# Layer 0 of a two-layer gated transformer: the slot schedule of its attention rewritten on all four engines, and the first steps of the last feed-forward reordered

## The reference

```
x = x + tanh(g_xattn[0]) * xattn0(layernorm(x), ctx)     # 16 heads of 16, 77 keys, this is "layer 0" below
x = x + tanh(g_ffn[0])   * moe(layernorm(x))             # 8 experts, top 2
x = x + tanh(g_xattn[1]) * xattn1(layernorm(x), ctx)     # 16 heads of 64
x = x + tanh(g_ffn[1])   * ffn(layernorm(x))             # amax of the input, quantize, gelu, amax of hidden, quantize

def xattn0(query, key_value):
    q, k, v = heads(query @ Wq + bq), heads(key_value @ Wk + bk), heads(key_value @ Wv + bv)
    attn = softmax(clip(q @ k.T / sqrt(16), -1e4, 1e4))
    return merge(attn @ v) @ Wo + bo
```

## Time and profile before

| | |
|---|---|
| median of 3 runs | 1161.29 us (1160.04 to 1161.42) |
| the profiled execution | 1163.3 us, of which the span from first to last instruction 1161.2 us |
| layer 0's attention in the span | 0 to about 246 us |
| the last feed-forward in the span | about 1015.6 us to the end |
| busy share of the span | TensorE 91%, VectorE 79%, ScalarE 72%, GpSimd 46% |

### The profile page before, as it was taken

The page is one execution under the profiler, slowest core; times in us unless marked ns, Lnnn a source line. Parts: engine busy times, 40 slices in busy tenths (PEclk is TensorE's granted clock), DMA queues, the critical chain, the costliest instruction groups (busy, mean ns, idle before and its releaser), DMA issues.

```text
span 1161.2 us, 26321 instructions
## 1 busy us (share of the span) xinstructions
PE 1057.4 (91%) x8919; PEld 775.3 (67%) x8919; DVE 916.9 (79%) x1960; ACT 834.7 (72%) x2382; POOL 539.4 (46%) x515
## 2 busy tenths in 40 slices
PE   6888888868969999999999999589999999889898
PEld 5666666645537777777777777357777777645477
DVE  5999999957845687666666667479999999789798
ACT  4988889836656456556556667378888888569896
POOL 5888888732252122122122111178889887500140
PEclk9999999979989999999999999889999999989899
DMA  6443334349672343333333335345252423010034
GB/s 150 118 128 110 110 110 133 123 128 284 189 206 61 53 137 90 118 101 121 124 104 120 121 115 161 112 127 161 68 158 67 154 74 92 28 38 0 1 119 137
DMA packets 128814, 132.12 MB, mean 114 GB/s; under 512 B 24792, under 2 KB 112973, under 8 KB 128557
## 3 DMA queue, kind: packets, MB, share of 16 engines
q1 hardware_dynamic: 119901, 112.17, 32.0%
q0 software_dynamic: 6480, 17.70, 5.5%
q10 hardware_dynamic: 2304, 0.59, 0.3%
HBM read 82.78 MB, written 47.64 MB: 112 GB/s over the span
## 4 chain that ended last, share of the span: by engine, by line
PE 57%; DVE 4%; ACT 4%; issue 2%; DMA 1%; POOL 1%; DVEq 0%; SPq 0%; ACTq 0%; POOLq 0%
PE exp_ps_h L1527 15%; PE exp_ps_y L1540 9%; PE a_ps_o L1953 9%; PE a_ps_sc L1937 8%; PE f_ps_h L2264 5%; PE exp_ps_y L1546 5%; PE a_ps_p L1924 3%; ACT exp_h L1590 2%; DVE f_hlo L2395 2%; PE exp_ps_x L1506 1%; PE f_ps L2447 1%; PE f_ps L2443 1%; PE f_ps_x L2255 1%; DVE all_xn L2404 1%; PE a_ps_x L1911 1%
## 5 line engine op out<-in xcount | busy, mean ns | idle before, releaser
L1590 ACT ACTIVATE exp_h<-exp_ps_h,exp_b_now 128x256 f32<-128x256 f32 (+1 forms) x320 | 124.7, 440 | 142.4 <-PE exp_ps_h L1527 142.4
L1491 POOL DMA_INDIRECT exp_xg<-xn,all_token_of x71 | 84.4, 1188 | 304.0 <-PE exp_ps_x L1506 288.5
L1527 PE MATMUL exp_ps_h<-exp_xhi,exp_w_now 128*128 128x256 bf16 (+1 forms) x1280 | 196.4, 263 | 5.9 <-DVE exp_xlo L1625 5.9
L1986 ACT ACTIVATE a_z<-a_ps_sc,a_nmx 128x77 f32<-128x77 f32 x512 | 159.3, 367 | 35.6 <-DVE a_nmx L2088 35.6
L1527 PE MATMUL exp_ps_h<-exp_xlo,exp_w_now 128*128 128x256 bf16 (+1 forms) x640 | 161.4, 263 | 0.0
L1703 DVE TENSOR_TENSOR exp_hlo<-exp_h,exp_hhi 128x512 bf16<-128x512 f32 (+1 forms) x160 | 99.4, 632 | 70.4 <-ACT exp_hhi L1597 68.5
L1540 PE MATMUL exp_ps_y<-moe_w2s,exp_hhi 128*128 x568 | 134.2, 379 | 1.3 <-DVE exp_y L1722 1.3
L1527 PEld LDWEIGHTS exp_ps_h<-exp_xhi,exp_w_now 128*128 128x128 bf16 x1280 | 120.6, 99 | 20.7 <-issue 8.3
L1986 ACT ACTIVATION_READ_ACCUMULATOR a_z<-a_ps_sc,a_nmx 128x1 f32 x512 | 127.0, 248 | 0.0
L1953 PE MATMUL a_ps_o<-a_v_now,a_phi 128*128 128x256 bf16 (+1 forms) x640 | 106.6, 272 | 2.3 <-DVE a_plo L2077 2.3
L1937 PE MATMUL a_ps_sc<-a_k_now,a_xhi 128*128 128x462 bf16 (+1 forms) x384 | 98.6, 341 | 3.4 <-DMA a_k_now<-fold_klo 2.2
(11 more groups left out here) (279 smaller groups left out, 2735.5 us busy)
## 6 DMA issues: line engine op xcount, KB each, us to landing
a_stage<-in_L_ffn_W_dram SPq DMA_DIRECT2D x64, 256.0 KB, 3.2
y_slots<-exp_y SPq DMA_DIRECT2D x71, 128.0 KB, 1.7
fold_k<-route_kst SPq DMA_DIRECT2D x16, 308.0 KB, 4.5
fold_v<-route_vst SPq DMA_DIRECT2D x16, 308.0 KB
exp_job_in<-fold_k SPq DMA_DIRECT2D x14, 352.0 KB, 3.3
exp_job_in<-fold_v SPq DMA_DIRECT2D x14, 352.0 KB, 3.3
a_x<-in_x_dram SPq DMA_DIRECT2D x32, 128.0 KB, 2.3
x<-a_xo SPq DMA_DIRECT2D x32, 128.0 KB, 1.7
```

The costliest lines, as they stand in the source:

```text
L1491: pool.indirect_dma_start(out=xg[:, v, u, :], out_offset=None, in_=xn_dram[:, :], in_offset=bass.IndirectOffsetOnAxis(ap=at.bitcast(U32), ...
L1527: mm = pe.matmul(hidden[:, i, f % 2, slots(j)], w1_now[:, v, k, hl, f * P:(f + 1) * P], xx[:, k, slots(j)], start=(q == 0), stop=(q == len ...
L1590: ins = act.activation(h[:, f, slots(j)], hidden[:, i, f % 2, slots(j)], ACT.Gelu_apprx_tanh, bias=b1_now[:, v, f:f + 1])
L1986: ins = act.activation(z[:, u, h * KEYS:(h + 1) * KEYS], ps_sc[:, j, (h - SB[j][0]) * KEYS:(h - SB[j][0] + 1) * KEYS], ACT.Exp, bias=nmx[: ...
```

## The change

In `attention`, what each engine does in slot T:

- TensorE turns x(T+1) first, then scores(T), then chunks 0 to 3 of tile T-2, output(T-3), queries(T+1), chunks 4 to 7, then the first part of the value products, chunks 8 and 9, and the other two parts. `part` cuts `turns` into three lists by the chunks they read: 7, 7 and 3 products. The queries are one slot ahead of their scores.
- ScalarE: ReLU and exponential, copy of chunks 0 to 3, queries(T+1), the other two copies, both splits, xn(T+2), attnT(T-2). The xn is a slot earlier than before, attnT too.
- VectorE: `turned` ahead of the largest, the largest ahead of xo.
- GpSimd: both remainders one slot later, at the slot's head and round `power`; the multiplication last.

In `ffn`: x's rounding starts before the reciprocal and the product that only the steps need (`steps_of` becomes `scale_of` and `step_of`); two products of group 0 come ahead of group 1's transposes; the constant for rounding is set in f1, and f3's first scaling starts before the output steps.

```diff
@@ attention @@
+    part = [[i for i in turns if blocks[i][0] // 4 == k] for k in range(3)]
@@ gpsimd, def slot @@
+                if has(T - 1):
+
+                    pool.wait_ge(s["hi_done"], 2 * T - 1)
+                    at, cols = (T - 1) // 2, slice(v * 512, (v + 1) * 512)
+                    pool.tensor_tensor(w1[:, at, 1, cols], stage[:, v, 0, :], w1[:, at, 0, cols],
+                                       ALU.subtract).then_inc(s["lo_done"], 1)
                 if has(T + 2):
                     power(T + 2, u)
+                if has(T - 1):
...
                 if has(T):
 
                     pool.wait_ge(s["xn_done"], T + 1)
                     pool.tensor_tensor(x[:, t, :], x[:, t, :], gbo[:, :], ALU.add).then_inc(s["xb_done"], 1)
-
-                    pool.wait_ge(s["hi_done"], 2 * T + 1)
...
@@ tensor @@
+            queries(0)
 
             def slot(T, t, b):
+                if has(T + 1):
+                    wait(pe, s["pT_done"], 3 * (T - 2))
+                    pe.wait_ge(s["qT_done"], T + 1)
+                    turn_x(T + 1)
                 if has(T):
                     pe.wait_ge(s["qT_done"], T + 1)
                     if t == 0:
@@ -454,40 +472,37 @@
                             mm = pe.matmul(ps_sc[:, j, g * PAIR:(g + 1) * PAIR], qT[lane, g, :], kblk[lane, b % 2, g, :],
                                            start=True, stop=True)
                     mm.then_inc(s["scores_done"], 1)
+                if T == 1:
+                    values(1, 0)
                 if has(T - 2):
                     if T == 2:
                         pe.wait_ge(s["kT_done"], 1)
+                    pe.wait_ge(s["norm_done"], T - 1)
+                    wait(pe, s["pT_done"], 3 * (T - 3) + 1)
+                    turn_p(T - 2, 0)
+                if has(T - 3):
+                    output(T - 3)
+                if has(T + 1):
+                    queries(T + 1)
+                if has(T - 2):
+                    wait(pe, s["pT_done"], 3 * (T - 3) + 2)
+                    turn_p(T - 2, 1)
+                    wait(pe, s["xo_done"], T - 2)
+                    if t == 2:
+                        pe.wait_ge(s["v_done"], (T - 2) // TPB + 1)
+                    pe.wait_ge(s["pT_done"], 3 * (T - 2) + 1)
+                    attend(T - 2, part[0])
+                    pe.wait_ge(s["qT_done"], min(T + 2, TILES))
+                    wait(pe, s["pT_done"], 3 * (T - 3) + 3)
                     turn_p(T - 2, 2)
+                    pe.wait_ge(s["pT_done"], 3 * (T - 2) + 2)
+                    attend(T - 2, part[1])
+                    pe.wait_ge(s["pT_done"], 3 * (T - 2) + 3)
+                    attend(T - 2, part[2]).then_inc(s["pv_done"], 1)
@@ scalar @@
             normal(0, 0, 0)
+            normal(1, 1, 1)
             act.wait_ge(queries_in, 32)
+            short_queries(0)
 
             def slot(T, t, b):
                 u = t % 2
                 if has(T - 1):
                     zt = z[:, (T - 1) % NZ, :]
                     act.wait_ge(s["z_done"], T)
                     act.activation(zt, zt, ACT.Relu, scale=-1.0).then_inc(s["zc_done"], 1)
                     act.wait_ge(s["zc_done"], T)
                     act.activation(zt, zt, ACT.Exp, scale=-scale).then_inc(s["exp_done"], 1)
+                if T == 1:
+                    v_copy(1)
                 if has(T - 2):
                     wait(act, s["pv_done"], T - 2)
                     act.wait_ge(s["turned_p"], 3 * (T - 2) + 1)
                     act.activation(pT[:, 0:4, :].rearrange("p c t -> p (c t)"), ps_p[:, 0, :], ACT.Copy).then_inc(s["pT_done"], 1)
+                if has(T + 1):
+                    short_queries(T + 1)
                 if has(T - 2):
                     act.wait_ge(s["turned_p"], 3 * (T - 2) + 2)
                     act.activation(pT[:, 4:8, :].rearrange("p c t -> p (c t)"), ps_p[:, 1, :], ACT.Copy).then_inc(s["pT_done"], 1)
+                    act.wait_ge(s["turned_p"], 3 * (T - 2) + 3)
+                    act.activation(pT[:, RCH - 2:RCH, :].rearrange("p c t -> p (c t)"), ps_q, ACT.Copy).then_inc(s["pT_done"], 1)
                 if has(T):
 
                     act.wait_ge(piece_in[u], 32 * (T // 2 + 1))
                     act.activation(split["w1s"][:, T // 2, 0, u * 512:(u + 1) * 512],
                                    stage[:, u, 0, :], ACT.Copy).then_inc(s["hi_done"], 1)
                     act.activation(split["w2s"][:, 2 * T:2 * T + 2, 0:D],
                                    stage[:, u, 1, :].rearrange("p (g d) -> p g d", d=D),
                                    ACT.Copy).then_inc(s["hi_done"], 1)
+                if has(T + 2):
+                    normal(T + 2, u, (t + 2) % RING)
+                if has(T - 2):
+                    act.wait_ge(s["pv_done"], T - 1)
+                    wait(act, s["o_done"], T - 2)
+                    act.activation(attnT[:, :, :].rearrange("p g t -> p (g t)"), ps_v, ACT.Copy).then_inc(s["attn_done"], 1)
                 if T == 0:
                     v_copy(0)
                 if T == 1:
                     act.wait_ge(s["k_proj"], 2)
                     act.activation(kT[:, :, 1:B, :].rearrange("p g b k -> p g (b k)"), ps_p[:, 0:ng, 0:(B - 1) * KEYS],
                                    ACT.Copy).then_inc(s["kT_done"], 1)
@@ vector, def slot @@
+                if has(T + 1):
+                    turned(T + 1)
...
+                if has(T):
+                    dve.wait_ge(s["scores_done"], T + 1)
...
@@ ffn @@
                 integers(0, 0)
+                step_of(dve, s["step"], 0, x_scale, C.wi_step, in_step)
+                dve.memset(magic[:, :], MAGIC).then_inc(s["magic_set"], 1)
...
                 def step(g, v):
+                    ahead = 2 if isinstance(g, int) and g == 1 else 0
+                    if ahead:
+                        pe.wait_ge(s["lo_done"], 2)
+                        for f in range(ahead):
+                            product(0, 0, f)
...
-                act.wait_ge(s["magic_set"], 1)
+                act.wait_ge(C.magic_set, 1)
+                act.wait_ge(C.ffn_step, 8)
                 scale(0, 0)
+                act.wait_ge(C.ffn_step, 10)
```

More of the change, by code:

```diff
@@ L380, in slot @@
                                        ALU.mult).then_inc(s["norm_done"], 1)
[L381 to L386, removed]
             run(pool, slot)
@@ L427, in _, with queries, output, attend @@
             pe.wait_ge(keys_in, 16 * 3)
+            def queries(T):
+                pe.wait_ge(s["xnT_done"], T + 1)
+                for g in range(ng):
+                    for k in range(KD):
+                        mm = pe.matmul(ps_q[:, g * P:(g + 1) * P], wq[:, k, g * P:(g + 1) * P], xnT[:, k, :],
+                                       start=(k == 0), stop=(k == KD - 1))
+                mm.then_inc(s["q_done"], 1)
+            def output(T):
+                pe.wait_ge(s["attn_done"], T + 1)
+                for g in range(ng):
+                    mm = pe.matmul(ps_o, attnT[:, g, :], wo[:, g, :], start=(g == 0), stop=(g == ng - 1))
+                mm.then_inc(s["o_done"], 1)
+            def attend(T, some):
+                for i in some:
+                    c, q, half = blocks[i]
+                    j, g = q // ng, q % ng
+                    mine = [cc for cc, qq, _ in blocks if qq == q]
+                    n = min(P, ROWS - c * P)
+                    mm = pe.matmul(ps_v[32 * j:32 * j + 32, g * P:(g + 1) * P], vblk[0:n, T // TPB % 2, c, half, :], pT[0:n, c, :],
+                                   start=(c == mine[0]), stop=(c == mine[-1]))
+                return mm
             keys(0, 1, 0)
@@ L489, in slot @@
                 if T == 1:
-                    values(1, 0)
                     pe.wait_ge(s["v_rows_done"], 2)
@@ L671, in slot @@
                                              op1=ALU.add).then_inc(s["xo_done"], 1)
-                if has(T):
-                    dve.wait_ge(s["scores_done"], T + 1)
-                    dve.tensor_reduce(mx[:, :].rearrange("p (j x) -> p j x", j=LANES), scores, AX, ALU.max).then_inc(s["max_done"], 1)
-                if has(T + 1):
-                    turned(T + 1)
                 if has(T + 2):
@@ L2259, in step @@
                         pe.wait_ge(s["lo_done"], g * 2)
-                        for f in range(FCH):
-                            wait(pe, s["gelu_done"], (g - 1) * FCH + f - 3)
-                            part = [(k, xx) for k in range(KD) for xx in (xhi, xlo)]
-                            for i, (k, xx) in enumerate(part):
-                                mm = pe.matmul(ps_h[:, f % 4, :], C.wi_q[:, k, f * P:(f + 1) * P], xx[:, 1 - v, k, :],
-                                               start=(i == 0), stop=(i == len(part) - 1))
-                            mm.then_inc(s["h_done"], 1)
+                        for f in range(ahead, FCH):
+                            product(g - 1, 1 - v, f)
                 largest(0)
```

120 lines of the change are left out of this document (39 added, 81 removed).

## The result

The changed kernel takes 1176.98 us (median of 4 runs, 1175.12 to 1180.79) against 1161.15 before (4 runs, 1160.04 to 1161.42): ratio 1.0141, 95% interval 1.0130 to 1.0153: slower, and 0.5 us above the top of the forecast range (1163 to 1176.5). The profiled execution took 1175.12 us with a span of 1173.1; the one before took 1163.3 and 1161.2.

The account below looks back on a forecast made before the run. It took layer 0's slot to be bound by a three-engine ring through the clamp, replaced by a TensorE-ScalarE ring of 7.25 us; +9.0 + 2.2 + 0 - 1.1 = +10.1 on 1161.3 gave 1171.4 us, range 1163 to 1176.5.

Parts of the forecast that it names:

- The signs of the mechanism: Layer 0: z 7.2 to 7.3 apart, clamp 0.11 to 0.13, TensorE idle until xn, first values over 0.87, VectorE about 87%.
- The ring's term: Layer 0, ordinary slots: new ring of TensorE and ScalarE takes 7.25 us instead of 6.92; +9.0 us over the stretch.
- the upper bound of 7.40: Layer 0 slot: the ring's length with a longer TensorE wake-up or queries at 1.00 us.
- the hand-over from xn to the turn of x: Layer 0, ScalarE to TensorE at the ring's end: 0.07 us, as from split to remainder.
- The second rival: Layer 0 slower still: ring 7.40 (queries 1.00, TensorE wake-up, block tensors showing again), 1176 us; chance 0.10.
- The switches: TensorE in layer 0: each change between full and tiled layout costs 0.09 us, six a slot instead of four.
- the first rival: Layer 0: the switch into tiled layout is free, ring 7.05, total +4.1 us, 1165.4; chance 0.20.
- What bounded the kernel before: Layer 0 slot: a ring over three engines through z, ReLU, split, GpSimd's remainder and the clamp, 6.82 us.
- the fourth rival: Layer 0: only the freed lock counts, VectorE binds at 6.34 us a slot, -16.8 us, 1145.6; chance 0.03.
- Head, block slots, tail: Layer 0: head 0, slots building block keys and values cost nothing more, tail +2.2 us (bounds +1 and +3.2).
- The feed-forward: Last feed-forward: first half -1.2 us (bounds -0.7 and -1.5), second half +0.1, together -1.1.
- Sum: Whole kernel: +9.0 + 2.2 + 0 - 1.1 = +10.1 us on 1161.3, forecast 1171.4.

Follow-up runs that it names:

- experiment 2: The changed kernel with xn(T+2) moved ahead of the two splits on ScalarE; 1161.31 us, ratio 0.9984 to before, slot 6.70.
- experiment 3: The changed kernel with all 17 value products in one stretch behind chunks 8 and 9, splits still ahead of xn; 1161.08 us, ratio 0.9977 to before.
- experiment 1: The kernel before with GpSimd's new order alone; 1160.19 us, ratio 0.9968 to before, slot 6.81.
- experiment 5: The changed kernel with GpSimd's first scaling in f3 waiting for VectorE's first scaling; 1175.24 us, ratio 1.0116 to before.
- experiments 1 and 3 to 7: Includes 4: change, xn ahead of splits, values undivided, 1151.92 us; 6: before with the feed-forward's part alone, 1161.84; 7: 4 plus GpSimd behind VectorE in f3, 1149.85.

## Why the prediction was right in its direction, and which steps failed

**Direction and cause in layer 0: right.** The change makes a ring from TensorE's turn of x through ScalarE's splits back to it; experiment 2 opens it and the slot falls by 0.68. The signs of the mechanism are there: the clamp at 0.11, TensorE idle before the turn of x until xn, the splits directly behind the copy of chunks 8 and 9, 0.99 us from the start of the first value part to the next transposes. Two signs missed: the slot is 7.38, not 7.2 to 7.3, and VectorE's share is 82%, not 87%, since the slot is longer and its row of work shorter than I had them.

**The ring's term: too small by 0.13 us a slot.** Forecast 7.25, measured 7.38, near the upper bound of 7.40. By steps: TensorE's part with the hand-over to ScalarE 127.47 - 122.15 = 5.32 for 5.29; copy and splits 1.32 for 1.30; xn to the turn of x 129.52 - 128.79 = 0.73 for 0.59 + 0.07. The step that failed is the hand-over from xn to the turn of x: I took 0.07, that of ScalarE to GpSimd, and it is 0.14. The trace of before had a hand-over of this size, in the slot that I read:

```profile
126.18 0.58 ACT L549 ACTIVATE a_pT<-a_ps_p 128x512 f32<-128x512 f32 x1
...
126.91 1.02 PE L483 MATMUL a_ps_vo<-a_pT,a_vblk 128*32 128x128 f32 x14 [0.61 <-ACT a_pT L549]
```

0.15 from the copy's end (126.76), with TensorE idle for 0.61; the second stretch of values, after 0.17 idle, has 0.06 (120.84 + 0.38 to 121.28). The length of the idle time isn't what decides, though. In the tail of the change TensorE starts 0.05 after GpSimd's end with 0.65 of idle time (252.74 to 252.79) and 0.06 after ScalarE's with 0.47 (258.20 to 258.26); at the turn of x of experiment 3 it is 0.14 with 0.75 idle. In the rows of this attention that I compared, the hand-over is 0.14 to 0.15 where the wait that ends last is written behind another one for the same instruction (the turn of x, the first values), and 0.05 to 0.06 where it is the first or the only one. No run moved a wait to test this, so what makes the hand-over longer stays open.

The second rival, 7.40 and 1176 us, came nearest, but partly by luck. Its queries at 1.00 and its block tensors didn't show (queries 125.47 - 124.58 = 0.89, block slots below), its ring would have given +13.3 (29 x 0.48 less 0.6) where +11.4 came, and the feed-forward, +0.7 for -1.1, made up the difference.

29 slots at 7.38 instead of 7.25 are 3.8 us; the shorter slots at both ends of the stretch (7.27 and 6.70, then 7.26 and 6.55) give back 1.8 where I had 0.6. So +11.4 instead of +9.0.

**The switches: right.** By start and duration, the scores now start 0.08 before the end of the turn of x (122.48 against 122.56), the values 0.07 before that of the transposes (126.00 against 126.07); output, in the same layout, 0.16 before it (123.72 against 123.88). A switch into the tiled layout costs as much as one out of it, so the first rival's reason falls. The Trainium skill (TensorEngine Tiling (Array Packing), "Key Properties") says that changing the mode drains TensorE; these rows agree, for both directions.

**What bounded the kernel before: half right.** I had read one ring of 6.82 and there were two (experiment 1). The forecast didn't suffer, as the new ring was set against the measured 6.92, but the fourth rival, the freed lock alone at 6.34, could have been given nothing: the second ring stands in the timelines from which the earlier trace rows are taken, without a gap on ScalarE from ReLU to the copy of chunks 8 and 9.

**Head, block slots, tail: right.** 0 and -0.1. The slots with block tensors take 7.61 to 7.62 and 7.13 to 7.15, on average 7.38. The tail has +2.3 for +2.2, with 7.12 - 5.30 = 1.8 from the last transposes on, where I had 0.6 + 1.1.

**The feed-forward: wrong sign.** The first half gave -0.7, the weaker of its bounds. The clock rose at 1027.20 before and at 1038.52 after, 11.3 later, while the stage as a whole had started 11.14 later (1015.60 and 1026.74): 0.18 lost. At that point eight records of products were done instead of four, each worth 0.215 us at the high clock: 4 x 0.215 - 0.18 = 0.7. The early start itself bought nothing more, since the work lay at the low clock. The second half was forecast at +0.1, and here the step that failed is an overlap: VectorE's scaling was taken at 1.28 us, as if GpSimd's beside it cost nothing; it took 2.48, and the half +1.4. GpSimd's scaling had waited for `magic_set`, which came just as VectorE's began; after the change both wait for the same link of the chain, and GpSimd is there 0.14 us sooner. Here the lock decides against VectorE, whose reciprocal and output steps stand behind it. The Trainium skill (SBUF — State Buffer, "Who interferes with whom") puts it as "Issue order, not op shape, decides who blocks"; the rows of before, of after and of experiment 5 agree (1.28, 2.48, 1.28 us), and experiment 5 gives back 1.1 of the 1.4. I had used this rule for the clamp and not looked for it here.

**Sum.** With the measured terms of the touched parts, -0.1 + 11.4 + 2.3 - 0.7 + 1.4 = +14.3, and 1161.3 + 14.3 = 1175.6. That is 4.2 above the forecast: 2.4 from the ring, 1.3 from the scalings in f3 and 0.5 from the first half of the feed-forward. The median of 1176.98 is 1.4 above it, inside the spread of its four runs, and 0.5 above my range. The range's top was worked from "upper bounds in part", and left no room for two terms off in one direction together.

**Open.** The stages between, which the change doesn't touch, are 2.5 us shorter than in the profile of before. In the profiles of experiments 1 and 3 to 7 they are shorter too, by 1.1 to 2.6, in that of experiment 2 longer by 1.4. They thus vary by 4 us between executions that run the same code there, which is more than the 1.4 that the sum leaves; why wasn't tested. The cause of the 0.14 us hand-over at the turn of x, and why VectorE's row fits in 6.18 and not 6.34, are open as said above.

## What to carry to other kernels

Freeing a lock or shortening the ring you found pays only down to the next ring: follow the slot back from a second engine before you price it, since a row without gaps on ScalarE said here that another ring was level. When a step is moved a slot ahead, ask which instruction produces its input and what now stands ahead of that: xn behind two splits of 0.52 us made a ring 0.56 us longer than the old ones, and moving it ahead of them, together with undivided values, turned +1.4% into -1.0%. Where two engines that share a port are released by the same event, let the one whose result others wait for go first by an explicit wait.

## What the runs showed of the hardware

TensorE takes up another engine's result 0.14 to 0.15 us after its end at some places (xn 128.79 + 0.59, turn of x 129.52) and 0.05 to 0.06 after it at others (252.74 to 252.79), and not by how long it has been idle (0.63 and 0.65 us there). A head start of 0.14 us decided who held the shared port, and cost VectorE 1.20 us on an instruction of 1.28. A switch between full and tiled layout costs 0.08 to 0.09 us in either direction, by the profile's modelled ends. Value products that lie in two column groups took 1.06 us for seven, where all seventeen round four groups took 1.41.
